# Local attention in a float32 transformer kernel: PSUM banks dealt out anew, own-heads chain per step, value rows copied in two halves

## What is computed

```python
def _L0_xattn_ref(x, cond, Wq, bq, Wk, bk, Wv, bv, Wo, bo):   # x, cond: B, C=64, T=512
    q, k, v = (W @ x + bq), (W @ cond + bk), (W @ cond + bv)   # pointwise over T, 8 heads of 8
    k, v = pad(k), pad(v)                                      # 8 left, 7 right
    idx = arange(T)[:, None] + arange(16)[None, :]             # 16 keys for each query
    dots = einsum('bhdt,bhdtw->bhtw', qh, k_win) * 8 ** -0.5
    out = einsum('bhtw,bhdtw->bhdt', softmax(dots), v_win)
    return Wo @ out + bo                                       # gated, added to x
```

## Time and profile before

| | |
|---|---|
| median of 3 runs | 3335.3 us (3334.0 to 3343.16) |
| the profiled execution | 3344.26 us, its span 3342.5 us |
| PE busy | 3186.6 us (95%) |
| DVE, ACT, POOL busy | 1681.9 (50%), 1471.4 (44%), 1126.6 (34%) |
| `phase_local`, first score product to last output product | 26.16 to 344.3 us |

### The profile page before, as it was taken

How to read it: one execution, slowest core, us unless ns; L and a number is a source line. 1 busy time by engine, 2 the same in 40 slices (tenths; PEclk the granted TensorE clock), 3 DMA queues, 4 the chain that set the end, 5 groups by cost and what they waited for, 6 DMA issues and landing times. The chain is left out here.

```text
span 3342.5 us, 55363 instructions
## 1 busy us (share of the span) xinstructions
PE 3186.6 (95%) x21704; PEld 2537.4 (76%) x21708; DVE 1681.9 (50%) x3572; ACT 1471.4 (44%) x3294; POOL 1126.6 (34%) x689
## 2 busy tenths in 40 slices
PE   8888999999999999999999979999999999999997
PEld 5666568888888888888854437888788878888885
DVE  5677444334333433333353566555655565556554
ACT  5666334444444444444322434444444434444443
POOL 6666323232223233322220113334333423334322
PEclk9999999999999999999999989999999999999999
DMA  3000121221212111112012102122111212221201
GB/s 106 2 2 2 42 82 62 65 76 58 70 57 77 63 64 63 64 64 64 20 60 85 38 16 105 64 70 87 58 66 67 77 64 69 65 69 66 74 32 58
DMA packets 56565, 199.92 MB, mean 60 GB/s; under 512 B 8976, under 2 KB 9744, under 8 KB 53008
## 3 DMA queue, kind: packets, MB, share of 16 engines
q1 hardware_dynamic: 56336, 196.76, 17.5%
HBM read 192.54 MB, written 4.19 MB: 59 GB/s over the span
## 5 line engine op out<-in xcount | busy, mean ns | idle before, releaser
L1754 POOL TENSOR_TENSOR h_wol<-h_ro,h_woh 128x1024 fp32r<-128x1024 f32 x128 | 314.5, 2457 | 612.9 <-ACT h_woh L1805 612.9
L1750 POOL TENSOR_TENSOR h_wql<-h_rq,h_wqh 128x1024 fp32r<-128x1024 f32 x128 | 309.0, 2414 | 501.7 <-ACT h_wqh L1800 501.7
L2251 DVE COPY h_tf<-ps 128x512 f32<-128x512 f32 (+1 forms) x256 | 142.5, 557 | 606.7 <-PE ps L2032 606.6
L2255 DVE TENSOR_TENSOR h_ol<-ps,h_oh 128x512 fp32r<-128x512 f32 x256 | 176.7, 690 | 525.8 <-ACT h_oh L1858 525.8
L141 PE MATMUL ps<-h_woh,h_oh 128*128 128x512 f32 x1024 | 428.6, 419 | 5.9 <-DVE h_ol L2255 5.8
L141 PE MATMUL ps<-h_Xh,h_wqh 128*128 128x512 f32 x1024 | 415.5, 406 | 5.2 <-ACT h_sq L1844 1.9
L143 PE MATMUL ps<-h_woh,h_ol 128*128 128x512 f32 x1024 | 406.0, 397 | 0.0
L142 PE MATMUL ps<-h_wol,h_oh 128*128 128x512 f32 x1024 | 405.5, 396 | 0.0
L143 PE MATMUL ps<-h_Xh,h_wql 128*128 128x512 f32 x1024 | 401.8, 392 | 0.0
L142 PE MATMUL ps<-h_Xl,h_wqh 128*128 128x512 f32 x1024 | 400.3, 391 | 0.0
L1908 ACT ACTIVATE h_ex<-ps,h_mx 128x128 f32<-128x128 f32 x512 | 180.9, 366 | 270.9 <-DVE h_mx L2291 270.8
(11 more groups left out here) (298 smaller groups left out, 6302.2 us busy)
## 6 DMA issues: line engine op xcount, KB each, us to landing
h_rq<-in_L_Wq SPq DMA_DIRECT2D x128, 512.0 KB, 3.4
h_ro<-in_L_Wo SPq DMA_DIRECT2D x128, 512.0 KB, 3.4
h_rk<-in_L_Wkv SPq DMA_DIRECT2D x47, 512.0 KB, 3.3
h_craw<-in_ctxT SPq DMA_DIRECT2D x7, 1024.0 KB, 7.3
cnat<-in_ctx SPq DMA_DIRECT2D x4, 1024.0 KB, 8.6
t_craw<-in_ctxT SPq DMA_DIRECT2D x4, 1024.0 KB, 9.4
t_cn<-in_ctx SPq DMA_DIRECT2D x4, 1024.0 KB, 5.5
out_rows<-x SPq DMA_DIRECT2D x16, 256.0 KB, 2.5
```

Of the source, the lines that this page charges most:

```text
L1750: nc.gpsimd.tensor_tensor(wql[:, par], rq[:, par], f(wqh[:, par]), ALU.subtract).then_inc(m["p_wq"], 1)
L1754: nc.gpsimd.tensor_tensor(wol[:, par], ro[:, par], f(woh[:, par]), ALU.subtract).then_inc(m["p_wo"], 1)
L2251: nc.vector.tensor_copy(tf[:], ps[:, TBK, 0:PT]).then_inc(m["v_t"], 1)
L2255: nc.vector.tensor_tensor(by_head(ol), ps[:, AB, :].rearrange("p (b h t) -> p b h t", h=2, t=S), f(by_head(oh)), ALU.subtract).then_inc(m[ ...
```

## The change

The banks are dealt out anew: two for the scores (step g uses bank g % 2), one for `turn`, two for `values` (g % 2), one (OBK) for the output product alone; PB and PB+1 stay for the projections and value rows. The waits follow: `scores(g)` waits for the subtraction of g-2 instead of g-1; `output` waits no more for the value rows' copies, but for `gated_out` of the tile before; `queries` no more for `gated_out`; `values(g)` waits for the own heads of g-2 in every step. `own_heads` runs for one step at a time on half the width. `values_out` does two of its four copies in n2 and two in n3. `gated_out` moves from n3 to n1 of the tile after. The maximum gets a buffer of its own, twofold.

```diff
-                sv = ps[:, SB_, :].rearrange("p (n b k) -> p b n k", n=NB, b=2)
+                SB_, TBK, ZB, OBK, PB = 0, 2, 3, 5, 6
+                sv = [ps[:, SB_ + i, :].rearrange("p (n b k) -> p b n k", n=NB, b=2) for i in range(2)]
...
                             wait(pe, a_vx, j)
-                            wait(pe, a_ob, j - 2)
...
-                            wait(pe, v_sub, NQ * j + n)
+                            g = NQ * j + n
+                            wait(pe, v_sub, g - 1)
...
-                            if g % 2 == 0:
-                                wait(pe, v_oc, g // 2 - 1)
+                            wait(pe, v_oc, g - 1)
...
                         def output(j):
-                            pe.wait_ge(v_oc, 2 * (j + 1))
-                            pe.wait_ge(a_vx, min(j + 3, NTILE))
+                            pe.wait_ge(v_oc, NQ * (j + 1))
+                            wait(pe, a_ob, j)
...
-                                if n == 2 and j + 1 < NTILE:
-                                    values_out(j + 1)
+                                if n >= 2 and j + 1 < NTILE:
+                                    values_out(j + 1, (range(0, 2), range(2, 4))[n - 2])
...
-                                if n == 3 and j:
-                                    gated_out(j - 1)
+                                if n == 1 and j >= 2:
+                                    gated_out(j - 2)
...
-                        def own_heads(k):
-                            dve.wait_ge(s_av, 2 * k + 2)
-                            wait(dve, s_wo, k // 2 - 1)
+                        def own_heads(g):
+                            dve.wait_ge(s_av, g + 1)
+                            wait(dve, s_wo, g // NQ - 1)
...
-                                if g % 2 == 0 and g >= 4:
-                                    own_heads(g // 2 - 2)
+                                if g >= 3:
+                                    own_heads(g - 3)
```

More of the change, by code:

```diff
@@ L228, in phase_local @@
                 pr = sb("pr", [P, 2, 2, NB, KW], ctx=ph)
-                st = sb("st", [P, 2, 2, NB], ctx=ph)
+                st = sb("st", [P, 2, NB], ctx=ph)
+                mx = sb("mx", [P, 2, 2, NB], ctx=ph)
                 rc = sb("rc", [P, 2, 2, NB], ctx=ph)
@@ L405, in values @@
                                             last = nc.tensor.matmul(
-                                                ps[half, ZB + g % 4, col:col + S],
+                                                ps[half, ZB + g % 2, col:col + S],
                                                 vx[:, j % 2, 4 * n + 2 * q + b, hh, 2 * r:2 * r + 2].rearrange("p n o -> p (n o)"),
@@ L424, in _ @@
                         for _ in range(8):
-                            nc.tensor.matmul(ps[:, ZB + 3, :], tmp[:, 0, 0:P], tmp[:, 0], start=True, stop=True)
+                            nc.tensor.matmul(ps[:, OBK, :], tmp[:, 0, 0:P], tmp[:, 0], start=True, stop=True)
                         pe.wait_ge(l_w, 16 * 6)
@@ L430, in _ @@
                         values_of_context(0)
-                        occupy(ZB + 3, 2)
+                        occupy(OBK, 2)
                         value_rows(0)
-                        occupy(ZB + 3, 3)
+                        occupy(OBK, 3)
                         for j in range(NTILE):
@@ L487, in context_values_out, with values_out @@
                             last.then_inc(a_vp, 1)
[L489 to L492, removed]
+                        def values_out(j, ts):
+                            if ts[0] == 0:
+                                act.wait_ge(s_p, 4 * j + 4)
+                                wait(act, s_av, NQ * (j - 1))
+                            for t in ts:
                                 r = slice(32 * t, 32 * t + 32)
@@ L496, in values_out @@
                                     ps[r, PB:PB + 2, :].rearrange("p a (q i o) -> p (a q) i o", q=8, i=2))
-                            last.then_inc(a_vx, 1)
+                            if ts[-1] == 3:
+                                last.then_inc(a_vx, 1)
                         def powers(g):
@@ L512, in gated_out @@
                             wait(act, p_x, j - 1)
-                            nc.scalar.activation(tmp[:, j % 2], ps[:, PB, :], ACT.Identity, bias=bog[:],
+                            nc.scalar.activation(tmp[:, j % 2], ps[:, OBK, :], ACT.Identity, bias=bog[:],
                                                  scale=tg[:, 0:1]).then_inc(a_ob, 1)
@@ L529, in _ @@
                         act.wait_ge(p_z, 3)
[L530 removed]
+                        values_out(0, range(4))
                         for j in range(NTILE):
@@ L561, in _ @@
                         turned(STEPS - 1)
+                        gated_out(NTILE - 2)
                         gated_out(NTILE - 1)
@@ L570, in shares_sum @@
                             dve.wait_ge(a_e, g + 1)
-                            own(nc.vector.tensor_reduce(st[:, 1], ex[:, g % 2], AX_X, ALU.add))
+                            own(nc.vector.tensor_reduce(st[:], ex[:, g % 2], AX_X, ALU.add))
                             wait(dve, p_pr, g - 1)
-                            nc.vector.reciprocal(rc[:, g % 2], st[:, 1]).then_inc(v_rc, 1)
-                        def own_heads(k):
-                            dve.wait_ge(s_av, 2 * k + 2)
-                            wait(dve, s_wo, k // 2 - 1)
-                            z = ps[:, ZB + 2 * (k % 2):ZB + 2 * (k % 2) + 2, :].rearrange("p a (c h t) -> p (a c) h t", h=HH, t=TB)
-                            o = oc[:, k // 2 % 2, 2 * (k % 2):2 * (k % 2) + 2].rearrange("p n b c t -> p (n b c) t")
+                            nc.vector.reciprocal(rc[:, g % 2], st[:]).then_inc(v_rc, 1)
+                        def own_heads(g):
+                            dve.wait_ge(s_av, g + 1)
+                            wait(dve, s_wo, g // NQ - 1)
+                            z = ps[:, ZB + g % 2, :].rearrange("p (c h t) -> p c h t", h=HH, t=TB)
+                            o = oc[:, g // NQ % 2, g % NQ].rearrange("p b c t -> p (b c) t")
                             own(nc.vector.tensor_scalar(o, z[:, :, 0], hm4[:, 0:1], None, ALU.mult))
@@ L598, in _ @@
                                 dve.wait_ge(s_s, g + 1)
-                                own(nc.vector.tensor_reduce(st[:, 0], sv, AX_X, ALU.max))
-                                nc.vector.tensor_tensor(sc[:, g % 2], sv, bc(st[:, 0]), ALU.subtract).then_inc(v_sub, 1)
+                                own(nc.vector.tensor_reduce(mx[:, g % 2], sv[g % 2], AX_X, ALU.max))
+                                nc.vector.tensor_tensor(sc[:, g % 2], sv[g % 2], bc(mx[:, g % 2]), ALU.subtract).then_inc(v_sub, 1)
                                 if g >= 1:
@@ L625, in _ @@
                         shares_sum(STEPS - 1)
-                        own_heads(STEPS // 2 - 2)
-                        own_heads(STEPS // 2 - 1)
+                        for g in range(STEPS - 3, STEPS):
+                            own_heads(g)
         class FirstRows:
```

9 lines of the change are left out of this document (4 added, 5 removed).

## The result

The changed kernel takes 3318.14 us in the median of 4 runs (3317.22 to 3323.23), the kernel before beside it 3338.14 (4 runs). The ratio is 0.9944 with a 95% interval of 0.9929 to 0.9959: faster by 0.4 to 0.7%. The forecast was 3320.5, 14.8 less than before; the medians stand 18 to 20 apart. The profiled execution took 3323.23 us, its span 3321.4, 21.1 less than before.

A forecast was written before the change was run, and what follows sets the result against it. PE, busy 95% of the span, was taken as the bound, with 23.3 us of waits for ACT's copies as target. Plain tiles -9.1, statistics and scale tiles -2.9, ends -1.3, clock -1.5: -14.8 from 3335.3 gives 3320.5 us, range 3312 to 3335.

The forecast's parts named there:

- the likeliest case: Whole kernel: faster than before, chance 0.60, against 0.34 for the same and 0.06 for slower.
- Plain tiles: Eight plain tiles: 17.21 us each, 16.52 of PE work plus 0.69 waiting for ACT's row and POOL's heads; -9.1 us.
- b: Start of a step's band product on PE, from which other engines' times are counted; ACT's row was placed at b + 6.38.
- better start: The tile behind each scale tile: starts 0.2 us better, in three groups.
- Own heads: DVE, half-width own heads per step: 1.42 us, between bounds of 0.98 and 1.96; L585 at about 348 ns.
- Statistics and scale tiles: Three groups of the two, DVE late: statistics tile 17.5 us, scale tile 20.5; -2.9 us with the next tile's start.
- Both ends: Tile 0, values behind two copies: -0.4 us; tile 15, last output waiting for one step's own heads: -0.9 us.
- The clock: Four half-clock stretches at 1.48 us each: scale tiles keep three, the fourth goes; -1.5 us.
- Rival 1: DVE becomes the bound because half-width own heads cost the full 1.96 us; 3333 us, no change, chance 0.17.
- Rival 2: ACT's row 0.7 us later in n3 than placed, plain tile 17.9; 3330 us, no change, chance 0.13.
- Rival 3: Clock falls in most tiles, at small waits before scores and queries; 3353 us with 25 stretches, slower, chance 0.05.
- Rival 4: The removed wait is no wait, as PE lacked other input then; counted as part of rival 2's chance.

The follow-up runs named there:

- e6: e5 with POOL's masked heads dealt out 3, 3, 2 over n0 to n2 instead of 2, 3, 3; 3311.7 us, ratio 0.9919 to the kernel before.
- e4: The changed kernel with one score bank instead of two, scores waiting for the subtraction of the step before; 3316.1 us, ratio 0.9945 to the kernel before.
- e10: e3 with one filler product in front of the output product's waits in every tile; 3332.5 us, ratio 0.9994 to the kernel before.
- e3: The changed kernel with four value-row copies together in n2 and the output product's wait for them put back; 3336.3 us, ratio 1.0005 to the kernel before.
- e9: The changed kernel with the first instruction of own heads issued three times instead of once; 3343.2 us, ratio 1.0024 to the kernel before.
- e5: The changed kernel with ACT's row moved from n3 to n0, except for the scale tiles; 3315.5 us, ratio 0.9936 to the kernel before.
- e2: The kernel before with only the value-row copies split in two halves; 3391.6 us, ratio 1.0161 to the kernel before.
- e11: e7 with bn_stats spread over two tiles and three of the next phase's taken in n0 of tiles 12 to 14; 3305.9 us, ratio 0.9914 to the kernel before.
- e7: e6 with DVE's scale of the rows spread over n1, n2 and n3 of the scale tile; 3311.9 us, ratio 0.9917 to the kernel before.

## Why the prediction held, point by point

The time was right: 3318.1 against 3320.5, and faster, as the likeliest case said. Its parts are taken from the start times of tiles in the two profiled executions, slow stretches left out (a tile that had one is set to its undisturbed twin):

- *Plain tiles*, forecast -9.1: the eight took 146.8 before and 138.3 after, -8.5. The mechanism was right in both places. ACT's row ended at b + 6.48 instead of 6.38, and POOL's heads held n3 to 4.11. My 0.69 for both together came to 0.90, but 0.08 of that is no wait: I took the 1.90 from the band product to `queries` for the output product too, which opens at b + 1.98 (e6). So PE's work alone is about 16.6 a tile, not 16.52. The first plain tile of each group takes 17.08: it follows a longer n3, its row is less late, and n0 takes 5.08 instead of 5.43. This is the "better start" of the forecast, 0.34 instead of 0.2, and is counted here.
- *Own heads*: 348 and 286 ns were worked out, 351 and 289 measured. The row of 282 ns for 128 elements decided this rightly.
- *Statistics and scale tiles*, forecast 17.5 and 20.5, or -2.7 and +0.45 for three of each: measured 17.7 and 20.6, -1.8 and +0.8. The mechanism was right, 1.66 for the own heads as worked out; the wait for shares behind it was 0.68 instead of 1.0. I had left out a wait of 0.32 of the output product for own heads in the statistics tiles (4 times, with the one at the end).
- *Both ends*, forecast -1.3: tile 0 gave -1.0 and the end -0.1 (without its slow stretch, taken from e4, which has none there). In tile 15 the last output's wait fell by 0.54, from 2.15 to 1.61, as forecast, and the wait behind the statistics in n2 by as much in e4 (scores, 2.12 to 1.58). But the last turn, which waited for nothing before, now waits 0.90 for the shares, and this took most of it back. Before and after:

```profile
337.69 0.66 PE L387 MATMUL ps<-ident,pr 128*128 128x128 f32 x4
```
```profile
321.97 0.66 PE L388 MATMUL ps<-ident,pr 128*128 128x128 f32 x4 [0.90 <-POOL pr L312]
...
326.06 1.08 PE L418 MATMUL ps<-oc,wo 128*64 128x256 f32 x8 [1.61 <-DVE oc L585]
```

- *The clock*, forecast -1.5: this was the mis-sized term. It was -5.1 in the phase. Four stretches with a cost of about 6 went, one in tile 15 came; the three scale tiles kept a wait of 1.7 and a second one, and still had a full clock. The price for each was right, 1.48 against 1.5 in e10. Where they fall was not to be had from the longest wait alone: of the waits of 2.0 us at the output product, all four in before were followed by a slow stretch, but only two of the six in e3.

So without the clock the phase gave 10.6 where 13.3 was forecast, and with it 15.6 where 14.8 was. The two errors nearly cancel: that the total came so close is luck, and it looks better than its terms. The remaining 2 to 5 us of the measured difference lie in the start and in the unchanged rest.

*The rivals.* Rival 1 did not occur: own heads took 1.34 to 1.42 a step, not 1.96. e9 nearly gives its price, at 2.11 instead of 1.96. There the plain tiles lost 7.0 in all against the change where the rival had 3.9, the groups of statistics and scale tiles 11.3 where it had 8.5, and tile 15, which it left out, 4.4 (a longer slow stretch among it). Part of the excess is the 0.15 more a step: an estimate, if it counts in two to four steps of each of 16 tiles, is 5 to 10 us. Taken off the 22.5 of the phase or the 25 of the medians, it leaves 12 to 20 us over the change, which puts the rival at about 3330 to 3338: no change, as it said. What it had not said is how steep the price is: at 2.11 the change is slower than the kernel before (e9), so the mechanism that it named for "no change" could also have made it slower, and the prediction gave slower only to the clock. Rival 2 did not occur: the row was 0.1 later than placed, not 0.7. Rival 3 did not occur: no plain tile of the changed kernel had a slow stretch. Rival 4, that the removed wait was none, is refuted by the plain tile (17.42 against 18.35) and by e3, where the old order of the copies with the old wait put the time back.

The Trainium skill, "TensorE: Matmul & The Clock Gate", section "A second HAM failure mode: psum-queue depth-cycling", tells of a kernel that cycles through PSUM banks and idles briefly between groups, and whose clock swings. e10 and e3 use the same banks in the same order, and only e3, with idle times of 1.68 and 2.03 where e10 has 0.81 and 1.17, had slow stretches in tiles 1 to 14. So of the two things that the section names together, the idle time mattered here, by one profiled execution of each.

## What to carry to other kernels

When two products share a bank and a copy empties it, a bank of its own helps little unless the queue of the copying engine is cleared too, and splitting the copy helps only if nobody waits for the shared bank: the bank alone brought 0.34 us a tile, the split alone lost 55 us in all, both together brought 0.93 us a tile. Before a wait is removed, work out what the neighbours do in its shade: here ACT's row and POOL's heads, each hidden by the old wait, took back nearly half of it, and moving them (e5, e6) brought most of that half. Compare such a change by the length of its own phase, since a few us elsewhere can hide it.

## What the runs showed that I had not expected

- Waits of 3.9 us in each tile came with a slow stretch of the clock every time (e2), and these cost about as much again as the added waits. Waits of 1.7 once a tile never did in plain tiles (before, e3), and waits of 2.0 did in 6 cases of 10.
- One filler product, which computes nothing and took 0.87 us off the wait, kept the clock at 1.00 in tiles whose length it did not change (e10, in one profiled execution).
- The unchanged rest of the program took 2987.6 us in the profiled execution of e4 and 3000.2 in that of before. Over all 13 kernels its length follows PE's time at half clock in it: 38 us of it in e4, 41 in e3, e10 and e11, 55 in the change, 58 in e7, 64 in before, 68 in e2, with about 0.4 us of length for each us. So most of the spread goes with the clock. Why it falls more often in one execution than in another, in code that is the same, was not tested and stays open.

```profile
324.75:3312.30 2987.55, 2877.62 (x16904) 2312.05 (x16908) 1456.98 (x3113) 1252.41 (x2959) 901.60 (x468) 0.99 0.19 64
```
